# Reordering the full-height TensorE work of an attention kernel: g in front, whole output blocks between the halves of the transposes

## The chip, the cores and the metric

The kernel runs on one core of a Trainium2 chip. The metric is the device time of one execution in microseconds; lower is better. TensorE (PE in the profile) does the matmuls, ScalarE (ACT) the exponentials and some of the copies out of PSUM, VectorE (DVE) reductions, scalings and other copies, GpSimd (POOL) elementwise work between SBUF tensors, and the SyncE queue (SP) issues all large transfers.

## The reference, cut to what matters

The input x has the shape (64, 128, 128, 64). Each of the 64 x 128 rows of the picture is a sequence of 128 positions with 64 channels, and attention runs over the positions of one sequence:

```python
xn = (x - moving_mean) * rsqrt(moving_var + BN_EPS) * gamma + beta
q, k, v = xn @ Wq + bq, xn @ Wk + bk, xn @ Wv + bv
attn = softmax(einsum('bhid,bhjd->bhij', q, k) * d ** -0.5)
out = einsum('bhij,bhjd->bhid', attn, v) @ Wo + bo
return xn + out
```

## The kernel before

The parameters are folded at the start, so that a sequence needs four products on the main path: g, which is x times a folded weight (q and k in one matrix); the scores, g times x; u, the unnormalised probabilities times x; and the output, u times a folded weight of v and o. Everything is f32, and a matmul instruction of the program becomes two matmuls in the trace, except for the transposes, which stay one.

The 8,192 sequences are cut into 1,024 groups of 8. All engines run the same software pipeline (`pipeline`), whose `step(r, t, peeled)` handles two groups, an even one and an odd one, at several stages at once. The loop body holds four steps; the first and the last steps are written out. The order of the instructions inside a step is written by hand for each engine, and an engine executes its own in that order. Semaphores in rings of four (by the group's number modulo four) carry the dependences.

In one step TensorE does the following. In half-height form (64 of 128 rows, two matmuls side by side): `scores` of the groups 2t and 2t+1. In half-width form (64 of 128 columns): `probs_times_x` of 2t-4 and 2t-3. Then comes the full-height work, all 128 by 128: `transpose_probs` in two halves of four sequences for each of the groups 2t-2 and 2t-1, `project` (this makes g, one matmul of 512 columns) for 2t+4 and 2t+5, and `output` (four pairs of sequences) for 2t-4 and 2t-3. This text calls the halves of the transposes Ta, Tb (group 2t-2) and T'a, T'b (group 2t-1), the two projections P and P', and the two outputs O and O', of four pairs each.

Two PSUM tensors are single: `probsT_ps` holds one half of the transposes, so the next half may start only when the last has been copied to SBUF; `g_ps` holds one group's g. The copies are made by ScalarE for Ta, T'a (`keep_probsT` with half 0, L334) and T'b (half 1, L337), and by VectorE for Tb (`keep_probsT_b`, L516). ScalarE copies both g (`keep_g`, L346). The waits are these lines of `transpose_probs`:

```python
if half == 0:
    pe.wait_ge(probs_a_found[s], uses(r, n))
    if exists(r, n - 1, peeled):
        pe.wait_ge(probsT_b_kept[parts(n - 1)], uses(r, n - 1))
else:
    pe.wait_ge(probs_b_found[s], uses(r, n))
    pe.wait_ge(probsT_a_kept[s], uses(r, n))
```

`scores` of a group n reuses the PSUM tensor of group n-2 and so waits for `probs_b_found` of n-2, the last of the eight exponentials that ScalarE computes for that group (`exponentials`, L319: one activation for a sequence, and one read of the accumulator that gives its sum). ScalarE's first exponential of a group waits for `neg_top`, which VectorE derives from the scores (`find_max` L469, `find_shift` L479). VectorE's `scale` (L435) waits for the outputs, `o_made`.

Of the kernel before, what the change touches and what calls it, by code (L numbers as in the profile page):

```python
# [17 lines left out]
def build(nc: bass.Bass, x, gamma, beta, mean, var, wq, bq, wk, bk, wv, bv, wo, bo, out):  # L18
    B, H, W, C = x.shape
    PAIRS = GROUP // 2  # L20
# [10 lines left out]
    with ExitStack() as ctx:  # L31
# [71 lines left out]
        o_made = sem_ring("o_made")  # L103
        xT_kept = sem_ring("xT_kept")
        g_kept = sem_ring("g_kept")
        u_kept = sem_ring("u_kept")
# [41 lines left out]
        def uses(r, n):  # L148
            return count(r, n, SEMS, 1)
# [34 lines left out]
        def exists(r, n, peeled):  # L184
            return not peeled or 0 <= group(r, n) < N
# [117 lines left out]
        @block.scalar  # L303
        def _(act):
            act.wait_ge(dve_setup, ROW_VAR)
            nc.scalar.activation(col_tmp[:, 1:2], col_tmp[:, 0:1], ACT.Sqrt).then_inc(act_setup, 1)
            nc.scalar.activation(row_tmp[:, 1, :], row_tmp[:, 0, :], ACT.Sqrt).then_inc(act_setup, 1)

            def exponentials(r, n, peeled, rows):
                if not exists(r, n, peeled):  # L310
                    return
                s = parts(n)
                if 0 in rows:
                    act.wait_ge(neg_top_found[s], uses(r, n))
                    if exists(r, n - 4, peeled):
                        act.wait_ge(probsT_b_made[s], uses(r, n - 4))
                        act.wait_ge(sum_inverted[parts(n | 1)], uses(r, (n - 4) | 1))
                for q in rows:
                    last = nc.scalar.activation(probs[:, n % 4, q, :], score_ps[n % 2][:, q // PAIRS, q % PAIRS * W:(q % PAIRS + 1) * W],  # L319
                                                ACT.Exp, bias=neg_top[:, s, q:q + 1], accum_out=prob_sum[:, s, q:q + 1])  # L320
                    if q == HALF - 1:
                        last.then_inc(probs_a_found[s], 1)
                    if q == GROUP - 1:
                        last.then_inc(probs_b_found[s], 1)

            def keep_probsT(r, n, peeled, half):
                if not exists(r, n, peeled):
                    return
                s = parts(n)
                if half == 0:  # L330
                    act.wait_ge(probsT_a_made[s], uses(r, n))
                    if exists(r, n - 2, peeled):
                        act.wait_ge(u_made[parts(n - 2)], uses(r, n - 2))
                    nc.scalar.activation(probsT[:, n % 2, 0:HALF, :], probsT_rows, ACT.Copy).then_inc(probsT_a_kept[s], 1)  # L334
                else:
                    act.wait_ge(probsT_b_made[s], uses(r, n))
                    nc.scalar.activation(probsT[:, n % 2, HALF:GROUP, :], probsT_rows, ACT.Copy).then_inc(probsT_b_kept[s], 1)  # L337

            def keep_g(r, n, peeled):
                if not exists(r, n, peeled):  # L340
                    return
                s = parts(n)
                act.wait_ge(g_made[s], uses(r, n))
                if exists(r, n - 4, peeled):
                    act.wait_ge(scores_made[s], uses(r, n - 4))
                nc.scalar.activation(g[:, s].rearrange("p k w -> p (k w)"), g_ps[:],  # L346
                                     ACT.Identity, bias=g_bias[:, 0:1]).then_inc(g_kept[s], 1)

            def step(r, t, peeled):
                exponentials(r, 2 * t, peeled, range(0, 5))  # L350
                keep_probsT(r, 2 * t - 2, peeled, 0)
                exponentials(r, 2 * t, peeled, range(5, 6))
                keep_g(r, 2 * t + 4, peeled)
                exponentials(r, 2 * t, peeled, range(6, 8))
                exponentials(r, 2 * t + 1, peeled, range(0, 4))
                keep_probsT(r, 2 * t - 1, peeled, 0)
                exponentials(r, 2 * t + 1, peeled, range(4, 8))
                keep_probsT(r, 2 * t - 1, peeled, 1)
                keep_g(r, 2 * t + 5, peeled)

            pipeline(act, step)
# [191 lines left out]
        def _(pe):  # L553
            pe.wait_ge(dve_setup, FOLDED - 1)
            for i in range(3):
                last = nc.tensor.matmul(uo_ps[1][0:C, i:i + 1], w_raw[:, i, :], ab_col[:, 1:2], start=True, stop=True)
            last.then_inc(pe_setup, 1)
            pe.wait_ge(pool_const, POOL_CONSTS + 1)
            for i in range(3):
                for h in range(2):  # L560
                    last = nc.tensor.transpose(g_ps[0:C, (2 * i + h) * C:(2 * i + h + 1) * C], w_fold[:, i, :],
                                               ident[0:C, 0:C])
# [32 lines left out]
            def probs_times_x(r, n, peeled):  # L595
                if not exists(r, n, peeled):
                    return
                s = parts(n)
                pe.wait_ge(probsT_a_kept[s], uses(r, n))
                pe.wait_ge(probsT_b_kept[s], uses(r, n))  # L600
                if exists(r, n - 2, peeled):
                    if vector_adds(n - 2):
                        pe.wait_ge(y_found[parts(n - 2)], uses(r, n - 2))
                    else:
                        pe.wait_ge(attn_kept[parts(n - 2)], uses(r, n - 2))
                for k in range(PAIRS):
                    for h in range(2):
                        last = nc.tensor.matmul(uo_ps[n % 2][h * C:(h + 1) * C, k * W:(k + 1) * W], x_in[:, n % 8, PAIRS * h + k, :],  # L608
                                                probsT[:, n % 2, PAIRS * h + k, :], start=True, stop=True)
                last.then_inc(u_made[s], 1)  # L610

            def transpose_probs(r, n, peeled, half):
                if not exists(r, n, peeled):
                    return
                s = parts(n)
# [7 lines that stand above are left out]
                for q in range(HALF):  # L623
                    last = nc.tensor.transpose(probsT_ps[:, q * W:(q + 1) * W], probs[:, n % 4, half * HALF + q, :], ident[:])  # L624
                last.then_inc((probsT_a_made if half == 0 else probsT_b_made)[s], 1)

            def project(r, n, peeled):
                if not exists(r, n, peeled):
                    return
                s = parts(n)  # L630
                pe.wait_ge(xT_kept[parts(n | 1)], uses(r, n | 1))
                if exists(r, n - 1, peeled):
                    pe.wait_ge(g_kept[parts(n - 1)], uses(r, n - 1))
                nc.tensor.matmul(g_ps[:], w_g_all, xT[:, n % 8].rearrange("p k w -> p (k w)"),  # L634
                                 start=True, stop=True).then_inc(g_made[s], 1)

            def output(r, n, peeled, pairs):
                if not exists(r, n, peeled):
                    return
                s = parts(n)  # L640
                if 0 in pairs:
                    pe.wait_ge(u_kept[s], uses(r, n))
                for k in pairs:
                    last = nc.tensor.matmul(o_pairs[n % 2][:, :, k, :], uT[:, n % 2, k, :], w_o_all, start=True, stop=True)  # L644
                if PAIRS - 1 in pairs:
                    last.then_inc(o_made[s], 1)

            def step(r, t, peeled):
                scores(r, 2 * t, peeled)
                scores(r, 2 * t + 1, peeled)  # L650
                probs_times_x(r, 2 * t - 4, peeled)
                probs_times_x(r, 2 * t - 3, peeled)
                transpose_probs(r, 2 * t - 2, peeled, 0)
                project(r, 2 * t + 4, peeled)
                output(r, 2 * t - 4, peeled, range(0, 1))
                transpose_probs(r, 2 * t - 2, peeled, 1)
                output(r, 2 * t - 4, peeled, range(1, PAIRS - 1))
                project(r, 2 * t + 5, peeled)
                transpose_probs(r, 2 * t - 1, peeled, 0)
                output(r, 2 * t - 4, peeled, range(PAIRS - 1, PAIRS))  # L660
                output(r, 2 * t - 3, peeled, range(PAIRS))
                transpose_probs(r, 2 * t - 1, peeled, 1)

            pipeline(pe, step)
# [20 lines left out]
```

## Time and profile before

| | |
|---|---|
| device time, median of 3 runs | 4877.92 us |
| lowest and highest of the 3 | 4874.67 and 4880.36 us |
| the profiled execution: its device time | 4878.26 us |
| the profiled execution: its span | 4876.3 us |
| granted TensorE clock over the span | 1.000 |
| HBM traffic over the span | 165 GB/s |

The span is the time from the first to the last instruction in the trace. The profiled execution's own time is 1.96 us above its span and 0.34 us above the median. A time in a timeline is counted from the span's start.

### The profile page before, as it was taken

How to read it: one execution, taken by the hardware profiler on the slowest of the kernel's cores; microseconds unless marked ns; L12 is line 12 of the kernel's file. 1: busy time of each engine (PE TensorE's matmuls, PEld its weight loads, DVE VectorE, ACT ScalarE, POOL GpSimd, SP SyncE). 2: the span in 40 equal slices, each digit the busy share in tenths (PEclk: the TensorE clock that was granted, in tenths of full speed). 3: DMA queues.
4: the chain of work that ended last, by engine and by line, in shares of the span. 5: the costliest groups of instructions: out<-in, count | busy, mean ns of one | idle time of the engine just before them, and what ended most of it. 6: DMA issues, size and time to landing. Idle time of an engine off the chain costs nothing.

```text
span 4876.3 us, 170131 instructions
## 1 busy us (share of the span) xinstructions
PE 4836.4 (99%) x51224; PEld 4028.1 (83%) x51224; DVE 4404.0 (90%) x6946; ACT 4332.2 (89%) x18948; POOL 4511.8 (93%) x2824
## 2 busy tenths in 40 slices
PE   7999999999999999999999999999999999999999
PEld 5888888888888888888888888888888888888887
DVE  6999999999999999999999999999999999999998
ACT  6888888888889988888888888888898888888887
POOL 6999999999999999999999999999999999999997
PEclk9999999999999999999999999999999999999999
DMA  6888888888888888888888888888888888888886
GB/s 130 167 168 166 167 167 167 167 167 167 167 167 166 167 167 168 166 168 166 168 166 167 166 167 167 167 167 167 167 166 168 167 168 166 168 165 168 167 167 136
DMA packets 4294233, 806.24 MB, mean 165 GB/s; under 512 B 4294208, under 2 KB 4294208, under 8 KB 4294208
## 3 DMA queue, kind: packets, MB, share of 16 engines
q1 hardware_dynamic: 4294208, 805.93, 84.0%
q8 instruction: 13, 0.21, 0.0%
q14 instruction: 12, 0.10, 0.0%
HBM read 537.10 MB, written 268.44 MB: 165 GB/s over the span
## 4 chain that ended last, share of the span: by engine, by line
PE 99%; ACT 0%; DVE 0%; SPq 0%; issue 0%; DMA 0%; DVEq 0%
PE probsT_ps L624 21%; PE score_ps L591 21%; PE uo_ps L608 20%; PE uo_ps L644 19%; PE g_ps L634 18%; ACT probs L319 0%; DMA bias_col<-in_L_conv_bv 0%; ACT g L346 0%; ACT probsT L334 0%; PE uo_ps L572 0%; SPq L192 0%; SPq L190 0%; SPq L194 0%; DVE probsT L516 0%; DVE y L455 0%
## 5 line engine op out<-in xcount | busy, mean ns | idle before, releaser
L319 ACT ACTIVATE probs<-score_ps,neg_top 128x128 f32<-128x128 f32 x8192 | 2916.8, 385 | 474.8 <-DVE neg_top L479 474.8
L266 POOL TENSOR_TENSOR x_weighted<-x_in,row_weights 128x1024 f32<-128x1024 f32 x1024 | 2401.8, 2368 | 32.3 <-DMA x_in<-in_x 32.3
L319 ACT ACTIVATION_READ_ACCUMULATOR probs<-score_ps,neg_top 128x1 f32 x8192 | 1839.4, 225 | 0.0
L469 DVE TENSOR_REDUCE row_stat<-score_ps 128x8 f32<-128x1024 f32 x1024 | 1250.7, 1221 | 211.1 <-PE score_ps L591 189.7
L288 POOL TENSOR_TENSOR y<-attn,x_scaled_rows 128x512 f32<-128x512 f32 x768 | 979.6, 1276 | 327.7 <-DVE attn L435 327.7
L624 PE MATMUL probsT_ps<-ident,probs 128*128 128x128 f32 x8192 | 1272.4, 278 | 3.9 <-ACT probsT L334 2.6
L644 PEld LDWEIGHTS uo_ps<-w_o,uT 128*128 128x128 f32 x8192 | 1075.1, 191 | 243.3 <-issue 242.8
L624 PEld LDWEIGHTS probsT_ps<-ident,probs 128*128 128x128 f32 x8192 | 925.5, 141 | 411.7 <-issue 363.1
L277 POOL TENSOR_TENSOR x_scaled_rows<-x_weighted,out_bias 128x512 f32<-128x512 f32 x1024 | 1196.9, 1192 | 0.0
L644 PE MATMUL uo_ps<-w_o,uT 128*128 128x128 f32 x8192 | 1164.4, 275 | 0.0
L634 PE MATMUL g_ps<-xT,w_g 128*128 128x512 f32 x2048 | 1053.4, 596 | 8.5 <-ACT g L346 5.0
L591 PE MATMUL score_ps<-xT,g 64*128 64x128 f32 x16384 | 1053.9, 278 | 1.4 <-ACT probs L319 1.3
L591 PEld LDWEIGHTS score_ps<-xT,g 64*128 64x128 f32 x16384 | 959.3, 188 | 90.1 <-issue 90.1
L608 PE MATMUL uo_ps<-probsT,x_in 128*64 128x128 f32 x16384 | 1007.6, 276 | 0.2 <-DVE y L455 0.2
L608 PEld LDWEIGHTS uo_ps<-probsT,x_in 128*64 128x64 f32 x16384 | 883.8, 137 | 62.6 <-issue 0.8
L346 ACT ACTIVATE g<-g_ps,g_bias 128x512 f32<-128x512 f32 x1024 | 745.1, 728 | 23.1 <-PE g_ps L634 23.1
L435 DVE TENSOR_TENSOR attn<-uo_ps,inv_sum 128x512 f32<-128x512 f32 x768 | 531.2, 692 | 151.5 <-issue 96.9
L489 DVE COPY uT<-uo_ps 128x512 f32<-128x512 f32 x1024 | 655.1, 681 | 1.4 <-PE uo_ps L608 1.4
L334 ACT ACTIVATE probsT<-probsT_ps 128x512 f32<-128x512 f32 x1024 | 628.5, 614 | 24.3 <-PE probsT_ps L624 4.3
L526 DVE STREAM_TRANSPOSE xT<-x_quads 128x1024 f32<-128x1024 f32 x512 | 631.5, 1234 | 6.6 <-DMA x_quads<-in_x 6.5
L498 DVE TENSOR_REDUCE row_stat<-x_weighted 128x16 f32<-128x1040 f32 x512 | 624.5, 1220 | 1.7 <-POOL x_weighted L266 1.7
L337 ACT ACTIVATE probsT<-probsT_ps 128x512 f32<-128x512 f32 x512 | 340.8, 666 | 1.0 <-PE probsT_ps L624 1.0
(67 smaller groups left out, 1382.9 us busy)
## 6 DMA issues: line engine op xcount, KB each, us to landing
x_quads<-in_x SPq DMA_DIRECT2D x4096, 64.0 KB, 2.2
x_in<-in_x SPq DMA_DIRECT2D x1024, 256.0 KB, 3.4
out<-y SPq DMA_DIRECT2D x1024, 256.0 KB, 2.4
norm_row<-in_L_conv_gamma SPq DMA_DIRECT2D x1, 32.0 KB, 3.7
norm_row<-in_L_conv_beta SPq DMA_DIRECT2D x1, 32.0 KB, 3.8
norm_row<-in_L_conv_moving_mean SPq DMA_DIRECT2D x1, 32.0 KB, 4.2
norm_row<-in_L_conv_moving_var SPq DMA_DIRECT2D x1, 32.0 KB, 4.4
norm_row<-in_L_conv_bo SPq DMA_DIRECT2D x1, 32.0 KB, 4.7
```

What stands on the lines that cost most here:

```text
L266: nc.gpsimd.tensor_tensor(x_weighted[:, n % 4, :, 0:2 * C].rearrange("p s (h c) -> p s h c", h=2), x_in[:, n % 8, :, None, :].broadcast_to ...
L277: nc.gpsimd.tensor_tensor(x_scaled_rows[:, n % 8], x_weighted[:, n % 4, :, 0:C], bias_b, ALU.add).then_inc(x_scaled[s], 1)
L288: nc.gpsimd.tensor_tensor(y[:, s], attn[:, s], x_scaled_rows[:, n % 8], ALU.add).then_inc(y_found[s], 1)
L319: last = nc.scalar.activation(probs[:, n % 4, q, :], score_ps[n % 2][:, q // PAIRS, q % PAIRS * W:(q % PAIRS + 1) * W], ACT.Exp, bias=neg_ ...
L346: nc.scalar.activation(g[:, s].rearrange("p k w -> p (k w)"), g_ps[:], ACT.Identity, bias=g_bias[:, 0:1]).then_inc(g_kept[s], 1)
L469: nc.vector.tensor_reduce(row_stat[:, s, :, NEG_MAX].rearrange("p (h k) -> p h k", h=2), score_ps[n % 2][:].rearrange("p h (k w) -> p h k ...
L489: nc.vector.tensor_copy(uT[:, n % 2], uo_ps[n % 2][:].rearrange("p (k w) -> p k w", k=PAIRS)) \
L591: last = nc.tensor.matmul(score_ps[n % 2][:, h, k * W:(k + 1) * W], g[half, s, k, :], xT[half, n % 8, k, :], start=True, stop=True)
L608: last = nc.tensor.matmul(uo_ps[n % 2][h * C:(h + 1) * C, k * W:(k + 1) * W], x_in[:, n % 8, PAIRS * h + k, :], probsT[:, n % 2, PAIRS * h ...
L624: last = nc.tensor.transpose(probsT_ps[:, q * W:(q + 1) * W], probs[:, n % 4, half * HALF + q, :], ident[:])
L634: nc.tensor.matmul(g_ps[:], w_g_all, xT[:, n % 8].rearrange("p k w -> p (k w)"), start=True, stop=True).then_inc(g_made[s], 1)
L644: last = nc.tensor.matmul(o_pairs[n % 2][:, :, k, :], uT[:, n % 2, k, :], w_o_all, start=True, stop=True)
```

## The change

On TensorE the whole projection P moves in front of Ta. All four pairs of O stand between Ta and Tb, where one stood; two of them stood between Tb and P', and one after T'a. All four pairs of O' stay between T'a and T'b. On ScalarE, g of 2t+4 is copied before the first half of the transposes of 2t-2 and not after it, both after six exponentials of group 2t (they were after six and after five); the copy of T'a stands after three exponentials of group 2t+1, and not after four. No instruction is added or removed. Nothing changes on VectorE, GpSimd or the transfer queue.

```diff
             def step(r, t, peeled):
-                exponentials(r, 2 * t, peeled, range(0, 5))
+                exponentials(r, 2 * t, peeled, range(0, 6))
+                keep_g(r, 2 * t + 4, peeled)
                 keep_probsT(r, 2 * t - 2, peeled, 0)
-                exponentials(r, 2 * t, peeled, range(5, 6))
-                keep_g(r, 2 * t + 4, peeled)
                 exponentials(r, 2 * t, peeled, range(6, 8))
-                exponentials(r, 2 * t + 1, peeled, range(0, 4))
+                exponentials(r, 2 * t + 1, peeled, range(0, 3))
                 keep_probsT(r, 2 * t - 1, peeled, 0)
-                exponentials(r, 2 * t + 1, peeled, range(4, 8))
+                exponentials(r, 2 * t + 1, peeled, range(3, 8))
                 keep_probsT(r, 2 * t - 1, peeled, 1)
                 keep_g(r, 2 * t + 5, peeled)
...
-            def output(r, n, peeled, pairs):
+            def output(r, n, peeled):
...
-                if 0 in pairs:
-                    pe.wait_ge(u_kept[s], uses(r, n))
-                for k in pairs:
+                pe.wait_ge(u_kept[s], uses(r, n))
+                for k in range(PAIRS):
                     last = nc.tensor.matmul(o_pairs[n % 2][:, :, k, :], uT[:, n % 2, k, :], w_o_all, start=True, stop=True)
-                if PAIRS - 1 in pairs:
-                    last.then_inc(o_made[s], 1)
+                last.then_inc(o_made[s], 1)
...
                 probs_times_x(r, 2 * t - 3, peeled)
+                project(r, 2 * t + 4, peeled)
                 transpose_probs(r, 2 * t - 2, peeled, 0)
-                project(r, 2 * t + 4, peeled)
-                output(r, 2 * t - 4, peeled, range(0, 1))
+                output(r, 2 * t - 4, peeled)
                 transpose_probs(r, 2 * t - 2, peeled, 1)
-                output(r, 2 * t - 4, peeled, range(1, PAIRS - 1))
                 project(r, 2 * t + 5, peeled)
                 transpose_probs(r, 2 * t - 1, peeled, 0)
-                output(r, 2 * t - 4, peeled, range(PAIRS - 1, PAIRS))
-                output(r, 2 * t - 3, peeled, range(PAIRS))
+                output(r, 2 * t - 3, peeled)
                 transpose_probs(r, 2 * t - 1, peeled, 1)
```

## Rows read from the trace of the kernel before

**Rows 1.** The page: busy time by engine, share of the span, instructions.

```profile
PE 4836.4 (99%) x51224; PEld 4028.1 (83%) x51224; DVE 4404.0 (90%) x6946; ACT 4332.2 (89%) x18948; POOL 4511.8 (93%) x2824
```

**Rows 2.** Timeline of TensorE over one step: start, duration, line, matmuls in the run.

```profile
2411.60 2.06 PE L591 MATMUL score_ps<-xT,g 64*128 64x128 f32 x32
2413.58 1.97 PE L608 MATMUL uo_ps<-probsT,x_in 128*64 128x128 f32 x32
2415.48 0.66 PE L624 MATMUL probsT_ps<-ident,probs 128*128 128x128 f32 x4
2415.97 1.02 PE L634 MATMUL g_ps<-xT,w_g 128*128 128x512 f32 x2
2416.84 0.38 PE L644 MATMUL uo_ps<-w_o,uT 128*128 128x128 f32 x2
2417.06 0.60 PE L624 MATMUL probsT_ps<-ident,probs 128*128 128x128 f32 x4
2417.49 0.61 PE L644 MATMUL uo_ps<-w_o,uT 128*128 128x128 f32 x4
2417.94 1.02 PE L634 MATMUL g_ps<-xT,w_g 128*128 128x512 f32 x2
2418.80 0.60 PE L624 MATMUL probsT_ps<-ident,probs 128*128 128x128 f32 x4
2419.24 1.28 PE L644 MATMUL uo_ps<-w_o,uT 128*128 128x128 f32 x10
2420.45 0.63 PE L624 MATMUL probsT_ps<-ident,probs 128*128 128x128 f32 x4
2421.01 0.83 PE L591 MATMUL score_ps<-xT,g 64*128 64x128 f32 x10
```

**Rows 3.** Timeline of ScalarE in the same step: idle time before the instruction in brackets.

```profile
2414.27 0.37 ACT L319 ACTIVATE probs<-score_ps,neg_top 128x128 f32<-128x128 f32 x1 [0.94 <-DVE neg_top L479]
...
2417.04 0.69 ACT L346 ACTIVATE g<-g_ps,g_bias 128x512 f32<-128x512 f32 x1
2417.62 0.36 ACT L319 ACTIVATE probs<-score_ps,neg_top 128x128 f32<-128x128 f32 x1
...
2419.68 0.63 ACT L334 ACTIVATE probsT<-probsT_ps 128x512 f32<-128x512 f32 x1
2420.16 0.41 ACT L319 ACTIVATE probs<-score_ps,neg_top 128x128 f32<-128x128 f32 x1
...
2421.19 0.43 ACT L319 ACTIVATE probs<-score_ps,neg_top 128x128 f32<-128x128 f32 x1
2421.44 0.27 ACT L319 ACTIVATION_READ_ACCUMULATOR probs<-score_ps,neg_top 128x1 f32 x1
```

**Rows 4.** Timeline of the last step, where no projection is left: TensorE, ScalarE and VectorE.

```profile
4862.32 0.66 PE L624 MATMUL probsT_ps<-ident,probs 128*128 128x128 f32 x4
...
4863.02 0.60 ACT L334 ACTIVATE probsT<-probsT_ps 128x512 f32<-128x512 f32 x1 [1.97 <-PE probsT_ps L624]
...
4863.76 0.63 PE L624 MATMUL probsT_ps<-ident,probs 128*128 128x128 f32 x4 [0.56 <-ACT probsT L334]
...
4864.42 0.69 DVE L516 COPY probsT<-probsT_ps 128x512 f32<-128x512 f32 x1 [1.30 <-PE probsT_ps L624]
...
4865.26 0.63 PE L624 MATMUL probsT_ps<-ident,probs 128*128 128x128 f32 x4 [0.43 <-DVE probsT L516]
```

**Rows 5.** Weight loads of the transposes and of g: busy us, mean ns of one.

```profile
L624 PEld LDWEIGHTS probsT_ps<-ident,probs 128*128 128x128 f32 x8192 | 925.5, 141 | 411.7 <-issue 363.1
...
L634 PEld LDWEIGHTS g_ps<-xT,w_g 128*128 128x128 f32 x2048 | 307.6, 190 | 14.3 <-issue 14.2
```

**Rows 6.** Line L591 in one step: duration ns least, median, most.

```profile
L591 PE MATMUL score_ps<-xT,g x32: 272/272/373, 2411.6 to 2413.4; 64*128 64x128 f32 x32
```

**Rows 7.** Timeline of TensorE: the first and the last full step's scores.

```profile
56.32 2.06 PE L591 MATMUL score_ps<-xT,g 64*128 64x128 f32 x32
...
4851.05 2.06 PE L591 MATMUL score_ps<-xT,g 64*128 64x128 f32 x32
```

## The prediction

> **What bounds the kernel now.** I read the busy shares first. TensorE is busy for 99% of the span, while each other engine has 7 to 11% of it free [rows 1]. So the time is the sum of what TensorE issues, and the question is whether it ever waits. For that the timeline is needed, at the size of one step. From the scores at 56.32 us to those at 4851.05 us full steps follow each other; divided by this step's 9.41 that is 509 steps, 9.42 on average [rows 7]. One step is all there is to understand: 0.01 us in it is 5 us of the time.
>
> The step goes from 2411.60 to 2421.01 [rows 2]. From start to start, and counted as in the kernel's description: scores 1.98, probabilities times x 1.90, Ta 0.49, P 0.87, the pair of O 0.22, Tb 0.43, two pairs 0.45, P' 0.86, T'a 0.44, five pairs 1.21, T'b 0.56. Two pairs take 0.45, so a pair takes 0.223 (I use 0.112 for a matmul), and five should take 1.12. They take 0.09 more, and T'b after them shows 0.63 where an unhindered half shows 0.60, so its run is 0.03 longer too. TensorE waits there for ScalarE's copy of T'a: that copy starts at 2419.68, at its place in ScalarE's order (the row names no idle time), takes 0.63 to 2420.31, and T'b starts 0.14 later, at 2420.45 [rows 2, 3]. This wait of 0.12 us is the only one that I find in the step. It is also where I got the price of a handover: 0.14 from the end of a copy to the first transpose that it releases.
>
> **The bare round trip of the single PSUM tensor.** In the last step there is no projection, so the transposes stand closer together, and TensorE does wait [rows 4]. Ta starts at 4862.32, ScalarE's copy at 4863.02, it ends at 4863.62, and Tb starts at 4863.76: 1.44 us between the starts of two halves with an idle ScalarE. Ta there follows another form of matmul, which costs it 0.06 (0.49 against 0.43 in the ordinary step [rows 2]). Through VectorE it is 4863.76 to 4865.26: 1.50 us. Start of a blocked half to start of the copy is 0.66. No order of the instructions makes these shorter. They are what the change has to be held against: whatever TensorE has to do between two halves must fill 1.4 to 1.5 us, the first half's own run included.
>
> **The room before and after.** Before: Ta to Tb 1.58, Tb to T'a 1.74, T'a to T'b 0.44 + 1.12 = 1.56 without the wait [rows 2]. All are above the round trip; the last loses 0.12 because ScalarE comes late. After: Ta to Tb is Ta and four pairs, 0.44 + 8 x 0.112 = 1.33. Tb to T'a is Tb and P', 0.43 + 0.86 = 1.29. T'a to T'b is 1.33. Every one of the three is below its round trip. P is taken out of the sequence that has to cover the copies, and 0.86 us of cover goes with it. A wait of 0.12 is removed and three are added.
>
> **The step after, worked out.** Zero is the first matmul of the scores; d is a wait of the second group's scores, which is found last.
> - P starts at 3.88 + d (2415.48 less 2411.60) [rows 2]. It is now the first after the half-width form, so its weight load isn't hidden. For Ta this cost 0.06 with a load of 141 ns; g's load takes 190 ns, 0.05 more [rows 5], so I take 0.11. The scores confirm it: 373 instead of 272 ns for the first of them [rows 6]. The unknown is bounded by 0.06 (as Ta) and 0.11. So P takes 0.97, and Ta starts at 4.85 + d.
> - P's matmuls end 1.02 + 0.11 after its start, at 5.01 + d. ScalarE has finished its six exponentials by then (the first is at 2.67 [rows 3], six at 0.343 end at 4.73), and waits. The copy of g starts 0.05 later (2416.99 to 2417.04 before), at 5.06 + d, and holds ScalarE for 0.58 (2417.04 to 2417.62) [rows 2, 3]. The copy of Ta is queued behind it and starts at 5.64 + d, though Ta is done at about 5.48 + d.
> - That copy takes 0.60 and the handover 0.14 [rows 4]: Tb starts at 6.38 + d. TensorE was ready at 4.85 + 1.33 = 6.18 + d. First wait: 0.20.
> - Tb to T'a is the bare trip through VectorE, 1.50: T'a at 7.88 + d. A blocked half runs 0.46 (0.43 and the 0.03 seen on T'b), so TensorE was ready at 6.38 + 0.46 + 0.86 = 7.70 + d. Second wait: 0.18.
> - ScalarE after Ta's copy (free at 6.13 + d) does two exponentials of group 2t and three of 2t+1, 5 x 0.343, and is idle from 7.84 + d. Its copy of T'a can start only 0.66 after T'a, at 8.54 + d. With 0.60 and 0.14, T'b starts at 9.28 + d; TensorE was ready at 7.88 + 0.46 + 0.89 = 9.23 + d. Third wait: 0.05.
> - T'b to the next scores is 0.56: 9.84 + d.
> - The exponentials of group 2t+1 that are left, five instead of four, come after the copy of T'a, which holds ScalarE for 0.48. The last starts at 8.54 + 0.48 + 4 x 0.343 = 10.39 + d. Its accumulator is read 0.25 later in 0.23 (the row has 0.27, at the end of a long run without a wait, in which the exponentials' own durations grow from 0.37 to 0.43 [rows 3]; soon after a wait I take 0.04 less), so the sum is there at 10.87 + d. Counted from the new scores this is 1.03, and with 0.11 to the weight load (0.14 less the 0.03 to the matmul) it is 1.14. The second group's scores begin at 0.99 (half of 1.98) and their load at 0.88. Before, the last exponential ended at 2421.71, 0.70 after the scores at 2421.01: the load could come at 0.81, and nothing waited [rows 2, 3]. Now it is 0.26 late; the load's lead of 0.11 is lost and 0.10 of exposed load added [rows 6]: d = 0.25.
>
> So the step is 9.84 + 0.25 = 10.09, I say 10.10, against 9.42: 0.68 us more. The sum is 509 x 0.68 = 346, and with the profiled execution's own 4878.26 (0.3 above the median) 5224 us. As terms of a step: +0.05 for g's exposed load, -0.12 for the wait removed, +0.43 for the three waits, +0.25 for the scores' wait; these give 0.61, and what is left is 0.02 or 0.03 for each blocked half's longer run (0.46 for 0.44) and rounding. The walk, not the list, is the sum.
>
> Edits at no cost: fewer pieces of O free VectorE's scaling of the even group earlier, which TensorE's chain doesn't see. VectorE's copy of Tb moves later, and its scaling of the odd group follows O', which ends about as long before the next scores as it did. VectorE's work is 4404 / 509 = 8.65 a step and GpSimd's 8.86 [rows 1], so both gain over a microsecond of free time. No transfer is moved; the queue waits for GpSimd and VectorE, which have time. Without that cover each 0.1 us in a step costs 51 us.
>
> On the exposed load there is a rule that says otherwise: the Trainium skill, "TensorE: Matmul & The Clock Gate", section "LDWEIGHTS (loading the stationary operand)", has the time of a weight load follow from its columns alone. Both loads have 128 columns, so by it g in front would cost what Ta cost. The rows have 141 and 190 ns for the two, and I go by them.
>
> **The rivals.**
> - *The scores don't wait* (d is 0): ScalarE gives the last exponentials in time, because its copy of T'a comes earlier than I have it or the tail is shorter. The step is 9.84, the time 4878 + 509 x 0.42 = 5092 us. It decides at 0.26 us of reserve in ScalarE's tail. For it: ScalarE has 0.94 idle in a step [rows 3]. Against: that idle time is before the even group's first exponential, the wrong place.
> - *The copies fit* (the other side, faster): the halves' round trip is covered by 1.29 to 1.33 us of work, for instance because the copies release TensorE before the end that the trace shows, and ScalarE's new order takes the 0.12 away. The step is 9.41 - 0.12 + 0.05 = 9.34, the time 4878 - 41 = 4837 us. It decides at a round trip of 1.3 us. Against: two measured trips, 1.44 and 1.50, both with an idle engine.
> - *VectorE slips as well*: its copy of Tb is later in the step, and with the steps in which it also adds (`add_in_place`) it reaches `find_max` late by 0.2 us in half of them, which delays ScalarE's exponentials and the scores. That is 0.1 a step, 51 us, 5275 us. It decides when the odd scaling comes more than about 0.1 later than I have it.
> - *Load exposure as for Ta*: P costs 0.06 and not 0.11 on entry. The walk hangs on P's end, so all of it comes 0.05 earlier: 5224 - 25 = 5199 us. This is what the rule above would give.
>
> **How the numbers follow.** My forecast 0.66; scores don't wait 0.12; the rule's load 0.09; VectorE slips 0.07; the copies fit 0.05; about no change, if two of the waits fall together, 0.01. The predicted time is the first one's. Its own range is 5175 to 5260: copies of 0.57 to 0.63, three handovers uncertain by 0.02, and 0.05 on P. To hold 8 in 10 it is extended to the case without d: 5085 to 5265. A measurement of this kernel tells about 0.2% from no change; faster by more 0.05, within 0.01, slower by more 0.94.
>
> **What would show it.** In the changed kernel's timeline: starts of the halves 1.5, 1.5 and 1.4 us apart; idle time in front of Tb named by ScalarE's copy, in front of T'a by VectorE's, both over 0.1 us; ScalarE idle for about 0.3 before the copy of g and 0.7 before that of T'a; the scores in two runs of 16 with a wait for ScalarE's exponentials between; TensorE's busy share lower, its clock still 1.0. I am wrong if the halves stand 1.33 apart, or if the scores run as 32 in one piece.

## The result: 7.35% slower, and the profile after

The changed kernel takes 5238.58 us (median of 6 runs, 5237.01 to 5239.40) against 4879.76 us of the kernel before, measured beside it: a ratio of 1.0735, 95% interval 1.0724 to 1.0746. The forecast was 5224 us. Every run of either kernel lies within 0.11% of its median.

The page's line on busy time, after:

```profile
PE 5165.2 (99%) x51224; PEld 4056.3 (77%) x51224; DVE 4415.2 (84%) x6946; ACT 4367.3 (83%) x18948; POOL 4517.3 (86%) x2824
```

TensorE still shows 99%, as in [rows 1], though it issues the same 51,224 matmuls in 359 us more. The reader should distrust this share: the ends of matmuls are modelled, each lasts 272 ns or more where the next follows after 109, and so a wait of 0.2 us between two of them hardly leaves a gap. A little of it shows in a stretch of steps alone: between 1000 and 2000 us TensorE was busy for 1000.00 us before and is for 994.24 now, 0.06 us a step of the 0.70 that were added. The row of the weight loads fell from 83 to 77%, and the other engines fell by 6 or 7 points each: the same work in a longer span, so each has more idle time. One step of TensorE in the timeline, to be held against [rows 2]:

```profile
2406.43 2.35 PE L590 MATMUL score_ps<-xT,g 64*128 64x128 f32 x32
2408.70 1.97 PE L607 MATMUL uo_ps<-probsT,x_in 128*64 128x128 f32 x32
2410.60 1.12 PE L633 MATMUL g_ps<-xT,w_g 128*128 128x512 f32 x2
2411.57 0.60 PE L623 MATMUL probsT_ps<-ident,probs 128*128 128x128 f32 x4
2412.00 1.06 PE L642 MATMUL uo_ps<-w_o,uT 128*128 128x128 f32 x8
2413.09 0.63 PE L623 MATMUL probsT_ps<-ident,probs 128*128 128x128 f32 x4
2413.55 1.02 PE L633 MATMUL g_ps<-xT,w_g 128*128 128x512 f32 x2
2414.59 0.63 PE L623 MATMUL probsT_ps<-ident,probs 128*128 128x128 f32 x4
2415.05 1.06 PE L642 MATMUL uo_ps<-w_o,uT 128*128 128x128 f32 x8
2415.99 0.63 PE L623 MATMUL probsT_ps<-ident,probs 128*128 128x128 f32 x4
2416.55 2.35 PE L590 MATMUL score_ps<-xT,g 64*128 64x128 f32 x32
```

The step is 10.12 us, where it was 9.41. From start to start: the scores 2.27 (1.98 before), P 0.97 (0.87), Ta to Tb 1.52 with 1.33 of work in it, Tb to T'a 1.50 with 1.29, T'a to T'b 1.40 with 1.33. In all three the second half starts with a blocked load, which its 0.63 instead of 0.60 gives away. ScalarE in the same step, for [rows 3]:

```profile
2409.11 0.37 ACT L319 ACTIVATE probs<-score_ps,neg_top 128x128 f32<-128x128 f32 x1 [0.58 <-DVE neg_top L478]
...
2411.77 0.69 ACT L346 ACTIVATE g<-g_ps,g_bias 128x512 f32<-128x512 f32 x1 [0.45 <-PE g_ps L633]
2412.35 0.59 ACT L334 ACTIVATE probsT<-probsT_ps 128x512 f32<-128x512 f32 x1
...
2415.25 0.60 ACT L334 ACTIVATE probsT<-probsT_ps 128x512 f32<-128x512 f32 x1 [0.57 <-PE probsT_ps L623]
...
2417.11 0.39 ACT L319 ACTIVATE probs<-score_ps,neg_top 128x128 f32<-128x128 f32 x1
2417.36 0.23 ACT L319 ACTIVATION_READ_ACCUMULATOR probs<-score_ps,neg_top 128x1 f32 x1
```

ScalarE waits for P (0.45) and for T'a (0.57), and then TensorE waits for ScalarE. The weight loads of the scores that come next, in two pieces of 16:

```profile
2416.55 0.97 PEld L590 LDWEIGHTS score_ps<-xT,g 64*128 64x128 f32 x16 [0.17 <-issue]
2417.71 1.00 PEld L590 LDWEIGHTS score_ps<-xT,g 64*128 64x128 f32 x16 [0.19 <-issue]
```

The second group's loads begin 1.16 us after the first's, 0.12 after the odd group's last sum is there (2417.59). And who waited for whom, over the whole span (line, us in total, times, longest):

```profile
...
POOL y L288 <- DVE attn L434: 681.3, 513, 6.4
DVE probsT L515 <- PE probsT_ps L623: 564.8, 512, 2.3
ACT probs L319 <- DVE neg_top L478: 300.5, 512, 1.5
ACT probsT L334 <- PE probsT_ps L623: 294.7, 513, 2.3
ACT g L346 <- PE g_ps L633: 251.1, 512, 16.4
```

The second, fourth and fifth are new as waits of every step: the copiers stand ready before the transposes and g are done. So at these copies it isn't the copier's own load that makes the copy late. Such idle time alone doesn't prove that the trip sets the time, though: in experiment 5 it stays while no half is blocked. The proof is a distance between two halves that is longer than TensorE's work in it, with the 0.63 of a blocked half.

### The profile page after: what moved, and what is told of

Its sections match the earlier page's. It is cut to its first block, busy times and chain, and to the rows that moved or that the text cites. A ratio compares the mean times of both kernels' runs of the same rounds, so it can differ in the third digit from the quotient of the medians.

```text
span 5235.0 us, 170131 instructions
## 1 busy us (share of the span) xinstructions
PE 5165.2 (99%) x51224; PEld 4056.3 (77%) x51224; DVE 4415.2 (84%) x6946; ACT 4367.3 (83%) x18948; POOL 4517.3 (86%) x2824
## 4 chain that ended last, share of the span: by engine, by line
PE 99%; issue 1%; DVE 0%; ACT 0%; SPq 0%; DMA 0%; DVEq 0%
PE score_ps L590 22%; PE probsT_ps L623 22%; PE g_ps L633 19%; PE uo_ps L607 19%; PE uo_ps L642 17%; ACT probs L319 0%; DMA bias_col<-in_L_conv_bv 0%; ACT g L346 0%; PE uo_ps L571 0%; DVE row_stat L468 0%; SPq L192 0%; SPq L190 0%; SPq L194 0%; DVE probsT L515 0%; ACT probsT L334 0%
## 5 line engine op out<-in xcount | busy, mean ns | idle before, releaser
L319 ACT ACTIVATE probs<-score_ps,neg_top 128x128 f32<-128x128 f32 x8192 | 2883.5, 376 | 300.5 <-DVE neg_top L478 300.5
L319 ACT ACTIVATION_READ_ACCUMULATOR probs<-score_ps,neg_top 128x1 f32 x8192 | 1770.9, 216 | 0.0
L623 PEld LDWEIGHTS probsT_ps<-ident,probs 128*128 128x128 f32 x8192 | 899.0, 140 | 809.3 <-issue 785.2
L590 PE MATMUL score_ps<-xT,g 64*128 64x128 f32 x16384 | 1190.2, 284 | 9.0
L590 PEld LDWEIGHTS score_ps<-xT,g 64*128 64x128 f32 x16384 | 1014.3, 187 | 179.6 <-issue 176.6
L633 PE MATMUL g_ps<-xT,w_g 128*128 128x512 f32 x2048 | 1105.2, 622 | 8.0 <-ACT g L346 4.5
L642 PE MATMUL uo_ps<-w_o,uT 128*128 128x128 f32 x8192 | 1082.0, 275 | 0.0
L642 PEld LDWEIGHTS uo_ps<-w_o,uT 128*128 128x128 f32 x8192 | 995.2, 192 | 0.2 <-DVE uT L488 0.2
L334 ACT ACTIVATE probsT<-probsT_ps 128x512 f32<-128x512 f32 x1024 | 606.9, 593 | 294.7 <-PE probsT_ps L623 294.7
L515 DVE COPY probsT<-probsT_ps 128x512 f32<-128x512 f32 x512 | 353.9, 691 | 564.8 <-PE probsT_ps L623 564.8
```

The lines of the kernel that those rows point to most:

```text
L590: last = nc.tensor.matmul(score_ps[n % 2][:, h, k * W:(k + 1) * W], g[half, s, k, :], xT[half, n % 8, k, :], start=True, stop=True)
```

## The experiments

A step's length below is the mean over the 509 full steps: 9.42 before, 10.12 after. A time with a ratio is a median of 4 runs or more; one without (experiments 1, 3 and 5) is of a single run. The differences read from those are 73 us and more, where the kernel before spread over 7 us in all its runs.

**1. Either order alone.** The two halves of the change were crossed: TensorE's new order with ScalarE's old one, and the reverse.

```diff
--- changed kernel, ScalarE                       (e1_scalar_before)
-                exponentials(r, 2 * t, peeled, range(0, 6))
-                keep_g(r, 2 * t + 4, peeled)
+                exponentials(r, 2 * t, peeled, range(0, 5))
                 keep_probsT(r, 2 * t - 2, peeled, 0)
+                exponentials(r, 2 * t, peeled, range(5, 6))
+                keep_g(r, 2 * t + 4, peeled)
                 exponentials(r, 2 * t, peeled, range(6, 8))
-                exponentials(r, 2 * t + 1, peeled, range(0, 3))
+                exponentials(r, 2 * t + 1, peeled, range(0, 4))
                 keep_probsT(r, 2 * t - 1, peeled, 0)
-                exponentials(r, 2 * t + 1, peeled, range(3, 8))
+                exponentials(r, 2 * t + 1, peeled, range(4, 8))
```

> TensorE's order of the changed kernel with ScalarE's order of the kernel before (the copy of Ta after five exponentials, g after the sixth, the copy of T'a after four of the odd group). Theory (the handovers on single PSUM tensors and ScalarE's place in its order set the step): the copy of Ta is no longer behind that of g, so Tb comes 0.15 us earlier; but g's copy then starts only at 6.3 us of the step, P' (which needs g's PSUM tensor free) waits 0.5 us, T'a comes at 8.1, ScalarE reaches its copy only at 9.0, T'b waits 0.3 more, and the second scores don't wait. The step is about 10.3 us, the time 5320 us (5280 to 5360), so above the changed kernel's 5239. Rival (ScalarE's new order, g ahead of the copy of Ta, is what costs the time): near 5150 or below. Rival (only TensorE's order costs, ScalarE's is neutral): 5240.

Measured: 5322.1 us, at the point forecast. In its timeline P' waits for g's copy by name:

```profile
2409.94 0.63 PE L624 MATMUL probsT_ps<-ident,probs 128*128 128x128 f32 x4
2410.87 1.10 PE L634 MATMUL g_ps<-xT,w_g 128*128 128x512 f32 x2 [0.30 <-ACT g L346]
```

From Tb to P' it is 0.93 where the half alone takes 0.44. So ScalarE's new order as a whole isn't what costs: with TensorE's new order it saves 84 us.

The reverse has the kernel before, with ScalarE's lines of the change section's diff (their plus side).

> TensorE's order of the kernel before with ScalarE's order of the changed kernel. Theory: P stands behind Ta, its matmuls end at 5.4 us; the copy of g comes first on ScalarE, at 5.44, and that of Ta is queued behind it and starts at 6.0; Tb, which has one pair of outputs in front of it, waits 1.3 us (against 0.2 in the changed kernel). No wait in front of T'a and T'b, 0.1 in front of the second scores. The step is about 10.75 us, the time 5560 us (5520 to 5620). It says whether ScalarE's order could be changed without TensorE's. Rival (only the room between halves counts, ScalarE's order is neutral): TensorE's rooms are those of before, so about 4880 to 4950. Rival (ScalarE's new order costs some 0.2 us a step by itself): 4980.

Measured: 5559.85 us, the slowest of all. The wait is where it was put, in front of Tb, 1.52 us after the pair of O that stands before it:

```profile
2408.08 0.38 PE L643 MATMUL uo_ps<-w_o,uT 128*128 128x128 f32 x2
2409.60 0.63 PE L623 MATMUL probsT_ps<-ident,probs 128*128 128x128 f32 x4 [1.14 <-ACT probsT L334]
```

From the pair of O to Tb there is 0.22 of work, so the wait is 1.30. The same copy of g in front of the same copy of Ta costs 1.3 us a step here and 0.14 in the changed kernel (experiment 3). An order on one engine has no price of its own; it has one against the other engine's order.

**2. g back behind Ta.** TensorE does Ta, P, all of O, Tb, P', T'a, all of O', T'b, with ScalarE's old order.

```diff
--- changed kernel, TensorE                       (e3_g_behind)
-                project(r, 2 * t + 4, peeled)
                 transpose_probs(r, 2 * t - 2, peeled, 0)
+                project(r, 2 * t + 4, peeled)
                 output(r, 2 * t - 4, peeled)
```

> The changed kernel with P back behind Ta and ScalarE's order of before; so against the kernel before only the pairs of the outputs are moved: all four of O between Ta and Tb. Theory: Ta to Tb has 2.2 us of room and no wait; Tb to T'a has 1.30 against a trip of 1.50 and waits 0.20; T'a to T'b has 1.33 against 1.40 and waits 0.08 (0.12 before); the second scores don't wait. The step is 9.58 to 9.62 us, the time 4970 us (4950 to 4995). Rival (g in front is what costs, the outputs' place is neutral): 4880. Rival (the outputs' place is what costs nearly all): above 5150.

Measured: 4957.83 us, ratio 1.0161 (1.0144 to 1.0178), a step of 9.58. The starts:

```profile
2407.87 0.66 PE L624 MATMUL probsT_ps<-ident,probs 128*128 128x128 f32 x4
2408.36 1.02 PE L634 MATMUL g_ps<-xT,w_g 128*128 128x512 f32 x2
2409.23 1.05 PE L644 MATMUL uo_ps<-w_o,uT 128*128 128x128 f32 x8
2410.12 0.60 PE L624 MATMUL probsT_ps<-ident,probs 128*128 128x128 f32 x4
2410.55 1.02 PE L634 MATMUL g_ps<-xT,w_g 128*128 128x512 f32 x2
2411.59 0.63 PE L624 MATMUL probsT_ps<-ident,probs 128*128 128x128 f32 x4
```

Tb shows 0.60 and waited for nothing; T'a comes 1.47 after it and shows 0.63. So moving the outputs costs 79 us, and g's place with the order on ScalarE that goes with it the other 280. With the 5322.1 of experiment 1 these part into 364 for g's place under ScalarE's old order, less the 84 that the new order gives back.

**3. The queue on ScalarE: the copy of Ta in front of that of g**, all else as in the changed kernel.

```diff
                 exponentials(r, 2 * t, peeled, range(0, 6))
-                keep_g(r, 2 * t + 4, peeled)
                 keep_probsT(r, 2 * t - 2, peeled, 0)
+                keep_g(r, 2 * t + 4, peeled)
```

> The changed kernel with ScalarE's copy of Ta in front of that of g; all else is the changed kernel's. Theory: Ta's copy starts as soon as Ta is done and the wait in front of Tb falls from 0.20 to 0.08; g's copy comes 0.48 later than before its turn and TensorE's P' waits 0.19 for g's PSUM tensor; VectorE's copy of Tb runs meanwhile, so the wait in front of T'a falls from 0.18 to 0.02 (less 0.02); T'b as it was, the scores' wait of 0.29 stays. The step is 9.95 to 10.0 us, the time 5160 (5140 to 5185). It says what the place of g's copy in ScalarE's queue costs: 0.15 us a step. Rival (the copies of g and Ta are exchangeable, as both are needed): 5240.

Measured: 5165.85 us, a step of 9.99, 73 us less than the changed kernel's. Over the steps Tb now comes 1.38 after Ta (1.52 in the changed kernel), and T'a 1.51 after Tb (1.50): the wait in front of T'a is exchanged for one of 0.12 in front of P', which can start only when g's PSUM tensor has been copied, and 0.07 more for the run of P' itself. The place of g's copy accounts for 0.14 us of the 0.70.

**4. The wait of the scores.** The copy of T'a moves behind two more exponentials, into the time in which ScalarE was idle.

```diff
-                exponentials(r, 2 * t + 1, peeled, range(0, 3))
+                exponentials(r, 2 * t + 1, peeled, range(0, 5))
                 keep_probsT(r, 2 * t - 1, peeled, 0)
-                exponentials(r, 2 * t + 1, peeled, range(3, 8))
+                exponentials(r, 2 * t + 1, peeled, range(5, 8))
```

> The changed kernel with ScalarE's copy of T'a after five exponentials of the odd group and not three. ScalarE was idle for 0.57 us in front of that copy, which 1.7 exponentials fill, and only three are left behind it instead of five. Theory: the three waits in front of transposes stay as they are, and the wait of the second scores for the odd group's last exponential (0.29 us a step) goes away altogether: the step is 9.84 us, the time 5238 - 509 x 0.29 = 5090 us (5075 to 5115). Rival (the scores' longer run isn't a wait for the exponentials but a dearer form or load of their own): 5240. Rival (the copy of T'a now comes late and T'b waits longer by what the scores gain): 5200 or more.

Measured: 5104.57 us, ratio to the kernel before 1.0462 (1.0445 to 1.0479); 134 us less than the changed kernel. The scores take 1.98 again:

```profile
2405.78 0.63 PE L623 MATMUL probsT_ps<-ident,probs 128*128 128x128 f32 x4
2406.37 2.06 PE L590 MATMUL score_ps<-xT,g 64*128 64x128 f32 x32
2408.35 1.97 PE L607 MATMUL uo_ps<-probsT,x_in 128*64 128x128 f32 x32
```

It is 15 us above the point that I gave, within the range: the copy of T'a now starts 0.67 after T'a (2405.01 to 2404.34) with no idle time named, but takes 0.62, not 0.60, and T'b waits 0.02 or 0.03 longer (mean over the steps). A little of the second rival is true.

**5. Shorter copies.** The copies of Ta, T'a and Tb move half of the columns. GpSimd sets the SBUF tensor to zero once at the start, so for these three halves half of the columns is left out of the probabilities times x.

```diff
-nc.scalar.activation(probsT[:, n % 2, 0:HALF, :], probsT_rows, ACT.Copy).then_inc(probsT_a_kept[s], 1)
+nc.scalar.activation(probsT[:, n % 2, 0:HALF, 0:W // 2], probsT_rows[:, :, 0:W // 2], ACT.Copy).then_inc(probsT_a_kept[s], 1)
...
-nc.vector.tensor_copy(probsT[:, n % 2, HALF:GROUP, :], probsT_rows).then_inc(probsT_b_kept[s], 1)
+nc.vector.tensor_copy(probsT[:, n % 2, HALF:GROUP, 0:W // 2], probsT_rows[:, :, 0:W // 2]).then_inc(probsT_b_kept[s], 1)
```

> The changed kernel, but the copies of Ta, T'a (ScalarE) and Tb (VectorE) move only the first 64 of each 128 columns out of PSUM; the rest of the SBUF tensor is zeros from the start, so part of the probabilities times x is left out. TensorE's work is the same. Theory: a copy of half the columns takes about 0.44 us on ScalarE (from 0.60 at 512 columns and 0.36 for an exponential of 128) and 0.42 on VectorE (0.69 less half of 512 columns), so the round trips fall to about 1.25, below TensorE's 1.3: the wait in front of T'a goes away, those in front of Tb (g's copy is still first) and T'b are 0.05 or less. The scores' wait stays, since the exponentials behind T'a's copy are still five, at about 0.2. The step is 9.5 to 9.65 us, the time 4950 (4910 to 5010). Rival (the waits come from the order of the queues, not from the copies' duration): only ScalarE's two halves of 0.16 us are gained, 5239 - 509 x 0.16 = 5160 or more. Rival (VectorE's and ScalarE's copies aren't in the path at all): 5240.

Measured: 4912.55 us, a step of 9.49, at the low end of the range. The halves stand 1.33, 1.30 and 1.33 apart, which is TensorE's own work between them, and none shows 0.63:

```profile
2405.18 0.60 PE L624 MATMUL probsT_ps<-ident,probs 128*128 128x128 f32 x4
...
2406.51 0.60 PE L624 MATMUL probsT_ps<-ident,probs 128*128 128x128 f32 x4
...
2407.81 0.60 PE L624 MATMUL probsT_ps<-ident,probs 128*128 128x128 f32 x4
...
2409.14 0.60 PE L624 MATMUL probsT_ps<-ident,probs 128*128 128x128 f32 x4
```

The groups of the two copies by line, busy time and mean ns:

```profile
L335 ACT ACTIVATE probsT<-probsT_ps 128x256 f32<-128x256 f32 x1024 | 388.2, 379 | 190.0 <-PE probsT_ps L624 190.0
L516 DVE COPY probsT<-probsT_ps 128x256 f32<-128x256 f32 x512 | 217.0, 424 | 392.5 <-PE probsT_ps L624 392.5
```

Both copiers are still idle in front of the copies (190.0 and 392.5 us in all), though no half waits. ScalarE's took 0.38 and not 0.44, which shortens the trips more than I had it. TensorE's work is unchanged and 326 us are gone, so the rival in which the order of the queues alone makes the waits falls. Of the waits, that of the scores is left: with five exponentials behind the copy they take 2.14 us of the step.

**6. One handover, with and without an idle engine behind it.** Only VectorE's copy is halved, once in the changed kernel and once in that of experiment 4. In both the other columns hold the zeros of the start, not, as the expectation has it, earlier groups.

> The changed kernel, but only VectorE's copy of Tb is halved (64 of 128 columns of each sequence; the other columns stay from earlier groups, so part of the result is left out). ScalarE's copies are whole. Theory: the trip from Tb to T'a falls from 1.50 to about 1.23 us, below TensorE's 1.30; the wait of 0.18 and the blocked half's 0.03 go away, and since ScalarE is idle for 0.57 in front of T'a's copy, all behind it comes earlier by as much: the step falls by 0.20, the time is 5239 - 509 x 0.20 = 5135 us (5125 to 5155). Rival (the waits stand in a row, and what T'a gains is lost at T'b or at the scores): 5220 to 5240.

> The same half copy on VectorE in the kernel with ScalarE's copy of T'a after five exponentials (which took 5105). Theory: T'a again comes 0.20 us earlier, but here ScalarE has no idle time in front of T'a's copy (0.04 at most), so that copy can't start earlier, T'b waits as much longer, and the step gains 0.04 at most: 5105 - 20 = 5085 to 5105 us. So a handover's wait is worth what it says only where the next engine in the chain is idle. Rival (each wait is a term by itself): 5105 - 509 x 0.20 = 5003.

Measured: 5129.68 us (ratio to the kernel before 1.0521, 1.0504 to 1.0539) and 5099.88 us (1.0462, 1.0444 to 1.0479). The same shortened copy is worth 109 us in the one and 5 in the other by the medians, 104 and 0 by the ratios (the kernel before took 4875.44 us beside these two). ScalarE in the second:

```profile
2407.57 0.69 ACT L347 ACTIVATE g<-g_ps,g_bias 128x512 f32<-128x512 f32 x1 [0.17 <-PE g_ps L634]
2408.15 0.59 ACT L335 ACTIVATE probsT<-probsT_ps 128x512 f32<-128x512 f32 x1
```

That 0.17 is its only idle time from the first exponential of the step on, where the changed kernel has a second of 0.57. T'a is early, ScalarE isn't, and T'b takes the difference as its wait:

```profile
2410.21 0.60 PE L624 MATMUL probsT_ps<-ident,probs 128*128 128x128 f32 x4
...
2411.81 0.63 PE L624 MATMUL probsT_ps<-ident,probs 128*128 128x128 f32 x4
```

T'a to T'b is 1.60 here and 1.43 in experiment 4 (mean over the steps), while Tb to T'a fell from 1.50 to 1.33.

**7. The kernel before, with its one wait taken away.** ScalarE's copy of T'a one exponential earlier.

```diff
--- kernel before, ScalarE                        (e8_before_earlier_copy)
-                exponentials(r, 2 * t + 1, peeled, range(0, 4))
+                exponentials(r, 2 * t + 1, peeled, range(0, 3))
                 keep_probsT(r, 2 * t - 1, peeled, 0)
-                exponentials(r, 2 * t + 1, peeled, range(4, 8))
+                exponentials(r, 2 * t + 1, peeled, range(3, 8))
```

> The kernel before with ScalarE's copy of T'a after three exponentials of the odd group instead of four, nothing else. Theory: the wait of 0.12 in front of T'b goes away, but five exponentials are now behind that copy: the second scores' load, which had 0.07 of reserve, comes late by 0.02 to 0.1 and pays 0.1 for its exposed load. Both together are about zero: the step is 9.39 to 9.43, the time 4875 (4862 to 4890). It tests the price of one exponential moved from one side of the copy to the other in a kernel where TensorE's rooms suffice. Rival (the wait in front of T'b is all that matters): 4880 - 61 = 4819. Rival (the scores' wait is as large as in the changed kernel): 4960.

Measured: 4884.59 us, ratio 1.0012 (1.0003 to 1.0021). The wait in front of T'b is gone and the scores have one of about the same size:

```profile
2404.19 0.60 PE L624 MATMUL probsT_ps<-ident,probs 128*128 128x128 f32 x4
2404.72 2.20 PE L591 MATMUL score_ps<-xT,g 64*128 64x128 f32 x32
2406.86 1.97 PE L608 MATMUL uo_ps<-probsT,x_in 128*64 128x128 f32 x32
```

T'b shows 0.60 and is followed after 0.53, but the scores take 2.14 and not 1.98. One exponential, 0.34 us, is more than the reserve on either side of that copy.

**8. A version that uses the rooms.** Every room is held at or above its trip, as far as eight pairs of outputs allow.

```diff
--- kernel before                                 (e7_three_pairs)
 ScalarE
-                exponentials(r, 2 * t, peeled, range(0, 5))
+                exponentials(r, 2 * t, peeled, range(0, 6))
                 keep_probsT(r, 2 * t - 2, peeled, 0)
-                exponentials(r, 2 * t, peeled, range(5, 6))
+                exponentials(r, 2 * t, peeled, range(6, 7))
                 keep_g(r, 2 * t + 4, peeled)
-                exponentials(r, 2 * t, peeled, range(6, 8))
+                exponentials(r, 2 * t, peeled, range(7, 8))
 TensorE
-                output(r, 2 * t - 4, peeled, range(0, 1))
+                output(r, 2 * t - 4, peeled, range(0, 3))
                 transpose_probs(r, 2 * t - 2, peeled, 1)
-                output(r, 2 * t - 4, peeled, range(1, PAIRS - 1))
+                output(r, 2 * t - 4, peeled, range(3, 4))
                 project(r, 2 * t + 5, peeled)
                 transpose_probs(r, 2 * t - 1, peeled, 0)
-                output(r, 2 * t - 4, peeled, range(PAIRS - 1, PAIRS))
                 output(r, 2 * t - 3, peeled, range(PAIRS))
```

> A version meant to be faster than both: TensorE does Ta, P, three pairs of O, Tb, one pair, P', T'a, all of O', T'b; ScalarE six exponentials, the copy of Ta, one, the copy of g, one, four of the odd group, the copy of T'a, four, the copy of T'b, g. Theory: rooms of 1.97, 1.52 and 1.33 us against trips of 1.44, 1.50 and 1.40; only T'b waits, 0.08 instead of 0.12. The step is 9.38 us against 9.42, the time 4860 (4850 to 4872). Rival (the copies of Ta and g, which now start 0.1 to 0.15 later, hold up Tb or P'): 4880 to 4930.

Measured: 4853.42 us, ratio 0.9947 (0.9934 to 0.9961): faster than either kernel, by 0.53% than the one before, which is small but clear of the spread of the runs. Its halves in the timeline:

```profile
2402.64 0.65 PE L624 MATMUL probsT_ps<-ident,probs 128*128 128x128 f32 x4
...
2404.66 0.60 PE L624 MATMUL probsT_ps<-ident,probs 128*128 128x128 f32 x4
...
2406.18 0.60 PE L624 MATMUL probsT_ps<-ident,probs 128*128 128x128 f32 x4
2406.61 1.06 PE L644 MATMUL uo_ps<-w_o,uT 128*128 128x128 f32 x8
2407.56 0.63 PE L624 MATMUL probsT_ps<-ident,probs 128*128 128x128 f32 x4
```

Only T'b is blocked. Tb to T'a is 1.52 and just holds against VectorE's 1.50.

## Why the prediction was right

The mechanism, the places and the sign were right, and the time was 15 us low (5224 against 5239, within the main case's own range too).

- *P's exposed load.* 0.97 taken, 0.97 measured (2410.60 to 2411.57). P's run is 0.10 above the 0.87 of [rows 2], where Ta's in that place was 0.06 longer; in experiment 2, with P back behind Ta, P shows 0.87 again and Ta has the 0.06. The Trainium skill, "TensorE: Matmul & The Clock Gate", section "LDWEIGHTS (loading the stationary operand)", lets a load's time follow from its columns alone. By that rule P would have cost what Ta cost, and the measured 0.10 against 0.06 decides against it.
- *The trips.* 1.53, 1.50 and 1.40 forecast for the three distances, 1.52, 1.50 and 1.40 measured. Experiment 5 shows that they are made of the copies' duration, and experiment 6 that the waits aren't independent terms.
- *g's copy in front of Ta's* was in the walk as 0.16 (5.64 instead of 5.48) and is 0.14 by experiment 3.
- *The mis-sized term is d*, the wait of the second group's scores: 0.25 forecast, 0.29 to 0.30 measured (2.27 or 2.28 instead of 1.98), 0.04 x 509 = 20 us. The sum came 1.04 and not 1.03 after the scores' start, the load 0.12 and not 0.11 after it, and the second group's 16 loads took 1.00 and not 0.97 us. Tb came 0.01 earlier than forecast, which takes back 5 us; what is left is the 15. That the term is a wait for the exponentials is shown by experiment 4, where it vanishes.
- *Signs in the profile.* I had expected idle time in front of Tb and T'a named by the copies, and a lower busy share of TensorE. No such idle time is named and the share still reads 99%: the waits of 0.2 us lie almost wholly under the modelled ends of the matmuls. They show in the starts, in the 0.63 of blocked halves, and in the copiers' idle time. Only waits well above 0.2 us are named, and by less than they cost: in experiment 1 the 1.30 in front of Tb as 1.14, the 0.49 in front of P' as 0.30. ScalarE's idle time in front of the copy of g was 0.45 and not 0.3. Two slips lie in that figure. I had left out d: the copy started 5.34 after the scores and not 5.06. And I had let an exponential hold ScalarE for 0.34, where the read of its accumulator ends 0.48 after its start: ScalarE was busy until 4.89 and not 4.73. The second slip alone makes 0.57 out of the 0.7 in front of T'a's copy. Neither touches the sum, since both copies wait for TensorE.
- *The rivals.* The copies don't fit. VectorE didn't slip: `find_max` of the even group starts 1.21 us after the scores (2406.43 and 2416.55) in a step with `add_in_place` and in one without, where it was 1.20 before (2412.80 less 2411.60); over the steps of both traces it is 1.19 to 1.21:

```profile
2407.64 1.23 DVE L468 TENSOR_REDUCE row_stat<-score_ps 128x8 f32<-128x1024 f32 x1
...
2417.76 1.23 DVE L468 TENSOR_REDUCE row_stat<-score_ps 128x8 f32<-128x1024 f32 x1 [0.68 <-PE score_ps L590]
```

  That the scores might not wait was the right alternative to name: two exponentials moved on ScalarE make it true (5105 us, where I had 5092).

## What to carry to other kernels

Where a PSUM tensor is single, measure the bare trip (producer's run, copy, handover) in a place where nothing else hides it, such as the last turn of a pipeline, and hold every distance between two users against it; work that is moved out of that distance is paid for one to one once the distance is below the trip. Each wait is worth what it says only if the next engine in the chain is idle there: the same 0.2 us a step was worth over 100 us in one order and next to nothing in another. Change the orders of two engines that hand work to each other together, and look at what is left behind the moved instruction until the next step's first use, since the tail is where a gain is given back.

## What the runs showed of the hardware that I had not expected

In the step shown, a pair of half-height matmuls whose loads came late doesn't close up again: the two loads of a pair start 35 ns apart to the end of the second group, where it is 7 in the first. The 16 loads of the second group of scores took 1.00 us in the changed kernel against 0.97 for the first group's 16, so a late start costs its delay and 0.03 us more. The wide spacing isn't bound to a late start: it stands in the second group of 509 of the 511 steps with scores in the changed kernel's trace, but also in both groups of 124 of these steps in the kernel before, where the scores wait for nothing. What causes it there is open. And ScalarE's copy of 128x256 from PSUM took 379 ns, where the one of 128x512 took 593, less than the line through an exponential of 128x128 (0.36) had led me to expect. The line through the two copies would give 0.27 at 128 columns, so the exponential and the copy don't lie on one line.
